# State-space scan kernel: GpSimd weighs two state steps in one instruction, in place, in a shared ring of eight buffers

## The reference

```python
def step(h, inp):
    dt_t, B_t, C_t, u_t = inp
    dA = jnp.exp(dt_t[:, :, None] * A)
    h = dA * h + dt_t[:, :, None] * B_t[:, None, :] * u_t[:, :, None]
    y = jnp.einsum('bds,bs->bd', h, C_t)
    return (h, y)
...
dt = jax.nn.softplus(dt @ Wdt.T + bdt)
y = jnp.swapaxes(ys, 0, 1) + u * Dp
y = y * jax.nn.silu(z)
return y @ Wo.T
```

## Time and profile before

| what | value |
|---|---|
| median of 3 runs (lowest to highest) | 2650.12 us (2649.25 to 2652.75) |
| the profiled execution | 2652.19 us |
| its span, first to last instruction | 2650.4 us |
| busy: PE, DVE, POOL, ACT | 2367.8, 2057.3, 2047.8, 1563.2 us |
| scans (L893) | 512, 2283 ns each |
| products (L1030) | 512, 2360 ns each |
| mean granted TensorE clock | 0.951 of full speed |

### The profile page before, as it was taken

The page is one execution under the profiler, slowest core; times in us unless marked ns, Lnnn a source line. Parts: engine busy times, 40 slices in busy tenths (PEclk is TensorE's granted clock), DMA queues, the critical chain, the costliest instruction groups (busy, mean ns, idle before and its releaser), DMA issues. The chain is left out here.

```text
span 2650.4 us, 22739 instructions
## 1 busy us (share of the span) xinstructions
PE 2367.8 (89%) x6064; PEld 1052.7 (40%) x6064; DVE 2057.3 (78%) x2025; ACT 1563.2 (59%) x2433; POOL 2047.8 (77%) x1269
## 2 busy tenths in 40 slices
PE   6688988889888999999999999999998899999586
PEld 4233333333333333333343333333333344444364
DVE  4899999999999999988998999899989443333221
ACT  4676777777775667666666666666666233222132
POOL 4699999999997799988899888888889432321276
PEclk9799999999999999999999999999999999999798
DMA  7565455644556766666666666566666500100254
GB/s 232 191 212 204 157 181 203 215 170 142 173 184 215 245 230 232 232 222 215 222 235 222 214 224 226 207 219 226 224 231 205 179 21 9 36 10 9 65 113 64
DMA packets 216892, 464.88 MB, mean 175 GB/s; under 512 B 29436, under 2 KB 109122, under 8 KB 216770
## 3 DMA queue, kind: packets, MB, share of 16 engines
q1 hardware_dynamic: 204786, 455.30, 51.0%
q0 software_dynamic: 11264, 7.98, 1.9%
q10 hardware_dynamic: 720, 0.23, 0.0%
HBM read 440.00 MB, written 23.99 MB: 175 GB/s over the span
## 5 line engine op out<-in xcount | busy, mean ns | idle before, releaser
L893 DVE TENSOR_TENSOR_SCAN hh<-decays,psdB 128x1024 f32<-128x1024 f32 x512 | 1165.6, 2283 | 53.4 <-ACT decays L715 20.0
L1030 POOL TENSOR_TENSOR products<-hh,Clo 128x1024 f32<-128x1024 f32 x408 | 961.5, 2360 | 153.7 <-DVE hh L893 150.9
L454 PE MATMUL psY<-products,ident 128*128 128x512 f32 x1708 | 820.1, 604 | 90.2 <-POOL products L1030 54.9
L715 ACT ACTIVATE decays<-dt,Acur 128x508 f32<-128x508 f32 x1024 | 668.0, 708 | 5.9 <-DVE hh L893 5.5
L882 DVE TENSOR_TENSOR psdB<-psT,Blo 128x1024 f32<-128x1024 f32 x395 | 484.1, 1226 | 65.7 <-ACT psT L683 32.6
L454 PEld LDWEIGHTS psY<-products,ident 128*128 128x128 f32 x1708 | 320.3, 193 | 525.8 <-issue 369.4
L1458 DVE TENSOR_TENSOR ac<-sg,d_bank 128x512 f32<-128x512 f32 x135 | 92.8, 688 | 225.4 <-PE d_bank L1308 175.6
L434 PE MATMUL psW<-xnT,wcur 128*128 128x512 f32 x496 | 227.2, 600 | 34.9 <-ACT u L646 18.9
L1030 POOL TENSOR_TENSOR products<-hh,late 128x1024 f32<-128x1024 f32 x104 | 244.1, 2367 | 11.7 <-PE psY L454 11.7
L728 ACT ACTIVATE late<-psdB 128x512 f32<-128x512 f32 x153 | 90.6, 592 | 233.0 <-PE psT L502 177.8
L1034 POOL TENSOR_TENSOR products<-products 128x512 f32<-128x512 f32 x170 | 215.6, 1268 | 13.3
(11 more groups left out here) (215 smaller groups left out, 3035.2 us busy)
## 6 DMA issues: line engine op xcount, KB each, us to landing
Blo<-rows SPq DMA_DIRECT2D x280, 512.0 KB, 6.0
Clo<-rows SPq DMA_DIRECT2D x280, 512.0 KB, 5.2
late<-rows SPq DMA_DIRECT2D x104, 512.0 KB, 6.5
wcur<-taps_l SPq DMA_DIRECT2D x31, 512.0 KB
fw<-in_Wg SPq DMA_DIRECT2D x36, 256.0 KB, 5.6
fw<-in_Wu SPq DMA_DIRECT2D x36, 256.0 KB, 4.5
fw<-in_Wd SPq DMA_DIRECT2D x36, 256.0 KB, 5.1
disp<-fw SPq DMA_DIRECT2D x16, 528.0 KB, 7.8
```

Source lines behind the costliest of these rows:

```text
L454: ins = pe.matmul(psY[:, :], lhsT=ident[:, :], rhs=gg[k % NGB][:, j, :], start=False, stop=(k % NK == NK - 1 and j == last - 1))
L715: ins = act.activation(dA[k % NDA][:, j, :, 1:T], dt[i % 2][:, c, :, 1:T], ACT.Exp, scale=Acur[i % 2][:, s:s + 1])
L893: dve.tensor_tensor_scan(out=hh[k % NHB][:, :, :].rearrange("p c t -> p (c t)"), data0=dA[k % NDA][:, :, :, :].rearrange("p c q t -> p (c ...
L1030: ins = pool.tensor_tensor(gg[k % NGB][:, :, :], hh[k % NHB][:, :, :], tile(Clo, Chi, slot(i, s)), ALU.mult)
```

## The change

In the first half POOL now multiplies two steps at a time, at the odd step of each two: one instruction of 128 x 2048 that takes the states of both, with two neighbouring tiles of C, and writes the product over the states. `prod` is raised by two when it is done. States and products share one ring of eight buffers (`states`), in place of four and four. A scan waits for the sums of eight steps ago, and products no longer wait for sums. In the second half POOL still multiplies step by step, in place.

```diff
-NDA, NHB, NGB, NDB = 4, 4, 4, 2
+NDA, NHB, NDB = 4, 8, 2
...
-                        ins = pe.matmul(psY[:, :], lhsT=ident[:, :], rhs=gg[k % NGB][:, j, :], start=False, stop=(k % NK == NK - 1 and j == last - 1))
+                        ins = pe.matmul(psY[:, :], lhsT=ident[:, :], rhs=hh[k % NHB][:, j, :], start=False, stop=(k % NK == NK - 1 and j == last - 1))
...
-                    at_least(dve, prod, n + 1 - NHB)
+                    at_least(dve, red, n + 1 - NHB)
...
                 def weigh_states(i, k):
                     n, s = NSTEP * i + k, pair(i, k)
+                    arrived(pool, c_ld, i, k)
+                    if i < RING0 and k % 2 == 0:
+                        return
                     pool.wait_ge(scan, n + 1)
-                    arrived(pool, c_ld, i, k)
-                    at_least(pool, red, n + 1 - NGB)
-                    ins = pool.tensor_tensor(gg[k % NGB][:, :, :], hh[k % NHB][:, :, :], tile(Clo, Chi, slot(i, s)), ALU.mult)
+                    if i < RING0:
+                        j, b = (s - 1, Clo) if s < NPR else (s - 1 - NPR, Chi)
+                        at = states[:, 2 * ((k - 1) % NHB):2 * (k % NHB) + 2, :]
+                        pool.tensor_tensor(at, at, b[:, j:j + 2, :, :].rearrange("p n s t -> p (n s) t"), ALU.mult).then_inc(prod, 2)
+                        return
+                    at = hh[k % NHB]
+                    ins = pool.tensor_tensor(at, at, tile(Clo, Chi, slot(i, s)), ALU.mult)
```

Four smaller parts go with it. The residual input of the dense MoE (`xin`) is loaded into the first half of `soft` rather than into a tile of its own, at step 13 rather than 0, and ACT waits for `x1_ok` before it writes `soft` again:

```diff
-        xin = late[:, NSLG + NXW, :].rearrange("p (q d) -> p q d", q=G)
+        xin = soft[:, 0, :].rearrange("p (q d) -> p q d", q=G)
...
-                    if d == 0:
-                        sp.wait_ge(prod, NSTEP * RING0)
-                    at_least(sp, x1_ok, d)
+                    sp.wait_ge(dt_ok, FIRST + NF * d)
...
+                        if c == 0 and t >= FIRST and (t - FIRST) % NF == 0:
+                            act.wait_ge(x1_ok, (t - FIRST) // NF + 1)
```

```diff
-        dx = [[sb(f"dx{c}_{p}", [128, NCH, RW]) for p in range(2)] for c in range(2)]
+        NDX = 3
+        dx = [[sb(f"dx{c}_{p}", [128, NCH, RW]) for p in range(NDX)] for c in range(2)]
...
+                turn(0, 0)
+                for e in range(NE):
+                    turn(e, 1)
+                    up(e, 0)
+                    up(e, 1)
+                    if e + 1 < NE:
+                        turn(e + 1, 0)
+                    down(e, 0)
+                    down(e, 1)
```

More of the change, by code:

```diff
@@ L36 @@
 RING0 = FIRST - 2
-NSLG = NB + 3
+NSLG = NB + 4
 NXW = 3
@@ L158, in wave_phase @@
         fw = K["fw"]
-        decays, products = sb("decays", [128, 2 * NDA, TOK]), sb("products", [128, 2 * NGB, TOK])
+        decays, states = sb("decays", [128, 2 * NDA, TOK]), sb("states", [128, 2 * NHB, TOK])
         dA = [decays[:, 2 * b:2 * b + 2, :].rearrange("p s (q t) -> p s q t", q=G) for b in range(NDA)]
-        hh = [sb(f"hh{b}", [128, 2, TOK]) for b in range(NHB)]
-        gg = [products[:, 2 * b:2 * b + 2, :] for b in range(NGB)]
+        hh = [states[:, 2 * b:2 * b + 2, :] for b in range(NHB)]
         Bhi, Chi = (late[:, 2 * NPR * b:2 * NPR * (b + 1), :].rearrange("p (n s) t -> p n s t", s=2) for b in range(2))
@@ L170, in wave_phase @@
         zrow = fw[:, 4:7, :].rearrange("p s t -> p (s t)")[:, 0:NCH * RW]
-        w12 = [buf[:, :, :].rearrange("p s t -> p (s t)")[:, G * WA * b:G * WA * (b + 1)].rearrange("p (q a) -> p q a", q=G) for buf in (decays, products) for b in range(2)]
+        w12 = [buf[:, :, :].rearrange("p s t -> p (s t)")[:, G * WA * b:G * WA * (b + 1)].rearrange("p (q a) -> p q a", q=G) for buf in (decays, states[:, NHB:2 * NHB, :]) for b in range(2)]
         xg = [hh[p][:, 0, :].rearrange("p (q d) -> p q d", q=G) for p in range(NAB)]
@@ L543, in _ @@
                 condition(5)
+                hidden(6)
                 pre(0, "dt0")
-                pre(0, "dt1")
-                hidden(6)
                 turn_x(7)
                 condition(6)
+                pre(0, "dt1")
                 hidden(7)
@@ L928, in _ @@
                     place(g)
+                adapt(7)
                 first_dt(0)
+                place(7)
                 first_dt(1)
-                adapt(7)
-                place(7)
                 for b in range(NDA):
@@ L1020, in give @@
                     n, c, s = NSTEP * i + k, k // NK, pair(i, k)
+                    if i == 0:
+                        pool.wait_ge(scan, 1)
                     arrived(pool, b_ld, i, k)
@@ L1489, in sparse_phase @@
         psT, psH, psE = bank[0:2], bank[2:6], bank[6:8]
-        x_ld = [sem("x_ld0"), sem("x_ld1")]
+        x_ld, x_first = [sem(f"x_ld{p}") for p in range(NDX)], sem("x_first")
         picked, homed, weighted, trans, copied, upped, gelud, downed, evac, added = (
@@ L1498, in at_least, with last, sums @@
                 eng.wait_ge(sm, v)
[L1500 to L1503, removed]
+        def last(h):
+            return h == NHT * NE - 1
+        def sums(h, q, n):
+            return psH[q][:, 0:128] if last(h) else psE[h % NHT][:, 128 * q:128 * (q + n)]
         with nc.Block() as block:
@@ L1552, in up, with down @@
                         pe.matmul(psH[f][:, :], lhsT=wg[p][:, f * 128:(f + 1) * 128], rhs=dT[c][:, :], start=True, stop=True).then_inc(upped, 1)
-                def down(e, p, c):
-                    h = NHT * e + c
+                def down(e, c):
+                    h, p = NHT * e + c, e % 2
                     pe.wait_ge(gelud, CR + NF * (h + 1))
                     at_least(pe, evac, CR + h - 1)
-                    for q in range(4):
+                    for q in range(HC):
                         for f in range(NF):
-                            ins = pe.matmul(psE[c][:, q * 128:(q + 1) * 128], lhsT=ht[c][:, f, q * 128:(q + 1) * 128], rhs=wd[p][:, f, :], start=(f == 0), stop=(f == NF - 1))
-                    ins.then_inc(downed, 1)
-                def body(e, p, j):
-                    up(e, p, j, 0)
-                    up(e, p, j, 1)
-                    down(e, p, 0)
-                    down(e, p, 1)
-                experts(pe, body)
+                            ins = pe.matmul(sums(h, q, 1), lhsT=ht[c][:, f, q * 128:(q + 1) * 128], rhs=wd[p][:, f, :], start=(f == 0), stop=(f == NF - 1))
+                        if q == HC - 1 or last(h):
+                            ins.then_inc(downed, 1)
+                turn(0, 0)
[7 more added lines that the diff above has]
+                    down(e, 1)
             @block.scalar
@@ L1573, in _ @@
                 act.sem_inc(gelud, CR)
[L1575 to L1583 removed]
+                for h in range(NHT * NE):
+                    c = h % NHT
+                    at_least(act, downed, CR + h - 1)
+                    for f in range(NF):
+                        act.wait_ge(upped, CR + NF * h + f + 1)
+                        act.activation(ht[c][:, f, :], psH[f][:, :], ACT.Gelu).then_inc(gelud, 1)
             @block.vector
```

128 lines of the change are left out of this document (71 added, 57 removed).

## The result

The changed kernel takes 2748.14 us (median of 4 runs, 2746.19 to 2749.4) against 2650.37 for the kernel before on the same chip: 1.0368 times as long, 95% interval 1.0354 to 1.0382. The forecast was 2720, in a range of 2675 to 2755. The direction and the ring were right; the step that charged one clock fall of 1.7 us per iteration was too small, and the gain of the end stage did not come.

A forecast was written before the change was run, and what follows sets the result against it. A ring of POOL's products, PE's sums and ACT's decays was taken to bound the first half. 2652.2 + 74.1 (13 iterations at 5.7) - 4.3 (sparse stage) = 2722.0, hence 2720 as the median; range 2675 to 2755.

The forecast's parts named there:

- the ring: First half: DVE waits for ACT's decays, ACT for PE's sums, PE for POOL's products; 54.52 us per iteration before.
- one clock fall of 1.7 us per iteration: PE's sums behind a new wait run partly at 1.2 GHz; 1.7 us per iteration, 40% chance.
- Leg C: From ACT's copy of the finished sum through PE and the Silu block to the next scan 7's end; unchanged at 19.84.
- Without clock falls: POOL waits for the softplus but PE's clock holds: 3.98 us more per iteration, 2698 in all; no fall 20%.
- rival with the softplus in time and the clock holding: First half: POOL doesn't wait for the softplus, PE's clock holds; 2.35 us more per iteration, 2676 in all; 11%.
- the wait for the softplus: POOL's time_step in the first half waits 1.63 us for ACT's softplus, as dt1 stands behind two sums on PE.
- leg A: POOL's leg, from the end of scan 7 to the end of product 13; from 25.73 to 27.99 us.
- the rival of 2742: PE's clock falls at both new waits: 7.4 us more per iteration; more than one fall (above 2735) had 19%.
- The ring of eight, products in place: Frees scans and products of waits that hardly stand in the rows; put at nothing, either way.
- The move of x: New place for xin's load, with a longer ring of gates; put at nothing, 34 us if the cover failed.
- The adapter stage: Ends some us earlier on DVE, but the first x0 waits for transfers; put at nothing, at best 3 us.
- The sparse stage: Sparse experts at the end: POOL becomes the limit, first scatter about 1.9 us earlier; 4.3 us gained, between 0 and 6.

The follow-up runs named there:

- the kernel with the clock kept up: Changed kernel, with PE adding zeros twelve times ahead of the sums of steps 6 and 12 in the first half; 2695.5 us.
- that kernel: Changed kernel, with dt1 right behind dt0, softplus ahead of ACT's first sum copy, and zeros added ahead of the sum of step 12 alone; 2675.2 us.
- The kernel with later loads: Kernel with pairs at steps 8 to 11 alone, plus end-stage loads waiting until the scatters of three experts back have landed; 2640.9 us.

## Why the prediction was right, and where it was wrong

**The ring and its legs.** Right, and closely. Leg C was to stay at 19.84 and is 19.84. Without clock falls the prediction had 58.50 us per iteration and 2698 for the whole; the kernel with the clock kept up has 58.46 and 2695.5. Its rival with the softplus in time and the clock holding had 56.87 and 2676; that kernel has 56.89 and 2675.2. The double product was put at 4.51 and takes 4.52, the wait for the softplus at 1.63, and it is 1.52 where the clock holds.

That the totals agree as well as the rings is luck in part: 2698 and 2676 count on 4.3 us from the end stage, and the two kernels gain 5.7 and 6.0 us outside the 13 turns elsewhere, most of it in the second half, which was put at nothing. And one reading behind a right sum was wrong: "the saving pays for most of it". Step 6 adds 2.33 us to leg A and four pairs save 0.6. The rest is POOL's wait of 1.14 for scan 8 in the kernel before (445.59, shown above), where POOL was said to run "nearly without a gap": the pair of 6 and 7 ends so late that POOL waits for neither scan 8 nor scan 9. The three expectations for kernels with product 7 single and a pair behind it left this wait out again, and came out 0.9 to 1.3 us per iteration too short.

**TensorE's clock.** This is the mis-sized term: "For the new waits I take one such fall on the ring, 1.7 us" was 3.77 (62.23 - 58.46), 49 us over 13 iterations instead of 22. This is nearly all of the 28 us by which 2720 fell short: the 4.3 us that the end stage didn't give and the 5.9 that the second half gained almost cancel. Both waits bring the low clock. Ahead of 6 and 7 two sums take 5.40 instead of 3.70, and this goes on to POOL through dt1 and the softplus; ahead of 12 and 13 it is 5.13 instead of 3.70, and 6.78 every fourth time. I had weighed the fall at 450 to 454 against the stretch from 462 to 466 that kept 1.00, and put the difference down to a shorter wait there. The timeline of PE before doesn't bear that out, since both waits are of one length:

```profile
449.20 3.65 PE L463 MATMUL psW<-yg,wo 128*128 128x512 f32 x4 [1.45 <-ACT soft L666]
...
464.27 1.98 PE L454 MATMUL psY<-products,ident 128*128 128x512 f32 x4 [1.50 <-POOL products L1030]
```

Ahead of the first PE had made dt1 (eight rows), ahead of the second sums and L418; why only the first brought a fall stays open. The new waits are 3.7 and 3.9, more than twice the longest on POOL before, 1.7. Rows of shorter waits couldn't settle these, but the one fall, behind 1.45 us, spoke for the bound at both, 3.4, and so for the rival of 2742; more than one fall had 19% in all. By the sentence of the Trainium skill that was weighed ("TensorE: Matmul & The Clock Gate", Part 1, "the default state is throttled, and activity releases the throttle") both new waits were to bring the slow clock: the trace after agrees at both, 0.60 and 0.58.

**The ring of eight, products in place.** Nothing in the first half, right: 54.79 with all steps single. **The move of x** was costed at nothing, with a risk of 34 us the other way; by the time it gained about 10. **The adapter stage** was put at nothing, at best a gain of 3; the changed kernel reaches scan 7 of iteration 0 1.5 us later, and no run tried this part alone. **The sparse stage** was to give 4.3 and gave nothing. The first scatter does come earlier, 2499.6 - 2065.3 = 434.3 us after the last scan against 2500.3 - 2063.0 = 437.3 with the old stage (both all single). But the scatters of the eight experts are then further apart. The timeline of POOL in the changed kernel, and the DMA's share (the column before the last) in the stretch where the scatters' transfers should land:

```profile
2629.36 1.54 POOL L1555 DMA_INDIRECT out<-eos,home  x1 [0.30 <-issue]
2633.40 1.54 POOL L1555 DMA_INDIRECT out<-eos,home  x1 [2.50 <-DVE home L1632]
...
2646.34 1.54 POOL L1555 DMA_INDIRECT out<-eos,home  x1 [0.30 <-issue]
2653.30 1.54 POOL L1555 DMA_INDIRECT out<-eos,home  x1 [5.41 <-DVE home L1632]
```

```profile
2644.00:2648.00 4.00, 4.00 (x26) 3.02 (x25) 1.39 (x3) 0.61 (x2) 3.27 (x3) 1.00 0.39 38
2648.00:2652.50 4.50, 4.50 (x11) 1.90 (x10) 0.00 (x0) 3.19 (x6) 0.00 (x0) 1.00 1.10 297
```

I had read POOL's period of 16.95 as its own limit, from a place where no loads started beside the last scatters: SP issued loads from 2528.1 and from 2545.4, the last scatter between them was issued at 2538.7. DVE, freed of its waits, now finishes an expert just when the last scatters are on their way, which lets SP start the next rows and weights (from 2646.55), and the DMA engines carry 297 GB/s while POOL waits for eight rows of its own. The profile names DVE's `home` as the releaser; DVE waits for the same landing (its cast of `home` for two experts ahead needs these scatters done). The kernel with later loads shows that the loads are the cause. The stage before, at PE's pace, had kept the two apart.

## What to carry to other kernels

Before two steps are joined into one instruction, look at who waits for the first of them: the join saves a fixed cost (0.15 us here) but starts at the second input and delivers the first output late, and where a ring waits at that step both are paid each turn; the other six pairs cost nothing here, and gained next to nothing. A wait that becomes longer on TensorE (here 3.7 and 3.9 us) has a second price in the work behind it, so charge a clock fall at every such wait on the ring, not at one. Where the chain can't be made shorter, either move the small step that is late (dt1) ahead of the joined work, or keep single the few steps whose result is waited for.

## What the runs showed of the hardware

Zeros added on TensorE in a wait of 3.7 us, which left waits of 0.8 to 1.2, kept the granted clock at 1.00 (2.4 GHz) in the sums behind them and shortened the program by 2%. An elementwise product of 128x2048 on GpSimd takes 4.52 us, two of 128x1024 4.66: the fixed share of an instruction is small at this size. The last of eight scatters let the next expert start 6.96 us after its issue instead of 4.04 when loads ran beside them at 297 GB/s.
